# Fetched features and own parts copied to fixed places, and transfers moved, in a graph network on one Trainium2 core

## The reference

```python
def _agg(entity_emb, relation_emb, W, head, tail, edge_type):
    a_input = jnp.concatenate([entity_emb[head], entity_emb[tail]], axis=-1)
    e = jnp.sum(a_input @ W * relation_emb[edge_type], axis=-1)
    e = jax.nn.leaky_relu(e, LEAKY_SLOPE)
    m = jax.ops.segment_max(e, head, num_segments=n)
    ex = jnp.exp(e - m[head])
    alpha = ex / segment_sum(ex, head)[head]
    return segment_sum(entity_emb[tail] * alpha[:, None], head) + entity_emb
# twice: ent = l2_normalize(_agg(ent, ...)); res = 0.5 * res + ent
```

## Time and profile before

| | |
|---|---|
| median of 3 runs | 5385.7 us (5385.49 to 5385.82) |
| the profiled execution | 5347.59 us, span 5346.3 us |
| mean granted TensorE clock | 0.635 |
| busy: PE, DVE, ACT, POOL | 3116.6, 3511.7, 2114.8, 1815.5 us |
| stages (us of the span) | before the hops 0 to 1349, hop 0 to about 2710, hop 1 2763 to 4112, normalisation to 4142, GAT scores to 4203, GAT's loop 4245 to 4608, the rest to 5346 |

### The profile page before, as it was taken

The page is one execution under the profiler, slowest core; times in us unless marked ns, Lnnn a source line. Parts: engine busy times, 40 slices in busy tenths (PEclk is TensorE's granted clock), DMA queues, the critical chain, the costliest instruction groups (busy, mean ns, idle before and its releaser), DMA issues. The chain is left out here.

```text
span 5346.3 us, 64952 instructions
## 1 busy us (share of the span) xinstructions
PE 3116.6 (58%) x16252; PEld 2276.0 (43%) x16253; DVE 3511.7 (66%) x8740; ACT 2114.8 (40%) x5595; POOL 1815.5 (34%) x1836
## 2 busy tenths in 40 slices
PE   3288888867144444444533444444454388878877
PEld 0144444456143434343533343433343388734443
DVE  8888888823466666666845666666677498553444
ACT  0255555532344444444522222222232488522331
POOL 5000000070666666666026766666630000011210
PEclk6699999977555555555555555555555555588997
DMA  0000000030222222222011222222210300000000
GB/s 10 6 0 0 0 0 0 0 138 3 64 54 57 53 57 54 56 54 56 21 37 50 58 55 55 56 54 56 54 40 11 133 1 1 2 10 4 4 2 13
DMA packets 136619, 183.67 MB, mean 34 GB/s; under 512 B 48690, under 2 KB 110043, under 8 KB 135323
## 3 DMA queue, kind: packets, MB, share of 16 engines
q1 hardware_dynamic: 85404, 84.66, 5.8%
q0 software_dynamic: 50048, 77.77, 5.8%
q10 hardware_dynamic: 896, 18.10, 0.8%
HBM read 158.07 MB, written 22.34 MB: 34 GB/s over the span
## 5 line engine op out<-in xcount | busy, mean ns | idle before, releaser
L992 POOL DMA_INDIRECT adjacency<-dram_table,sorted_dst x1564 | 1565.6, 1001 | 1192.1 <-issue 484.9
L1016 PE MATMUL bank<-adjacency 128*128 x3520 | 779.3, 419 | 561.1 <-DMA adjacency<-dram_table,sorted_dst 298.4
L1016 PEld LDWEIGHTS bank<-adjacency 128*128 128x128 f32 x3520 | 759.1, 332 | 607.4 <-issue 607.4
L1061 ACT ACTIVATE adjacency<-adjacency 128x128 f32<-128x128 bf16 x1760 | 537.1, 394 | 56.7 <-issue 56.7
L1728 PE MATMUL bank<-adjacency,cheb_parts 128*128 128x512 f16 (+1 forms) x2100 | 437.5, 367 | 52.2 <-ACTq L95 31.4
L1088 DVE TENSOR_TENSOR adjacency<-adjacency,bank 128x2048 f32<-128x2048 f32 x110 | 251.6, 2287 | 306.5 <-remote 219.9
L1034 PE MATMUL bank<-ident,adjacency 128*128 128x128 f32 x440 | 149.5, 395 | 519.4 <-issue 519.3
L1048 ACT ACTIVATE adjacency<-adjacency 128x2048 f32<-128x2048 f32 x110 | 210.2, 1911 | 604.6 <-DVE adjacency L1088 603.0
L553 ACT ACTIVATE adjacency<-bank 128x400 f32 x590 | 296.9, 503 | 317.1 <-PE bank L525 312.0
L1997 POOL TENSOR_TENSOR cheb_y<-cheb_y,cheb_gain 128x512 f32<-128x512 f32 (+1 forms) x21 | 24.2, 1150 | 1154.7 <-DVE cheb_y L1913 1154.7
L522 PE MATMUL bank<-cell_hot,src_hot 128*128 128x400 f16 x1180 | 319.3, 353 | 74.2 <-DVE cell_hot L460 73.2
(11 more groups left out here) (448 smaller groups left out, 6754.2 us busy)
## 6 DMA issues: line engine op xcount, KB each, us to landing
adjacency<-dram_src_rows SPq DMA_DIRECT2D x440, 128.0 KB
adjacency<-dram_table,sorted_dst POOLq DMA_INDIRECT x1564
dram_adjacency<-adjacency ACTq DMA_DIRECT2D x1, 17600.0 KB, 44.4
adjacency<-dram_adjacency SPq DMA_DIRECT2D x1, 17600.0 KB, 46.1
dram_table<-adjacency SPq DMA_DIRECT2D x2, 1212.5 KB, 10.3
dram_nodes<-x_nodes SPq DMA_DIRECT2D x1, 800.0 KB, 4.5
x_nodes<-dram_nodes SPq DMA_DIRECT2D x1, 800.0 KB, 4.3
x_nodes<-in_x SPq DMA_DIRECT2D x1, 768.0 KB
```

Source lines behind the costliest of these rows:

```text
L992: pool.indirect_dma_start(ring[:, j % (RG * TG), :], None, dram["table"], bass.IndirectOffsetOnAxis(ap=S.dst_i[:, j:j + 1], axis=0)).then_ ...
L1016: ins = pe.matmul(sums[b % 2][:, s * W1:(s + 1) * W1], reach[:, b % 3, s, t, :], ring[:, bass.ds(at_r[s], TG), :][:, t, 0:W1], start=(t == ...
L1061: ins = act.activation(reach[:, b % 3, s, t, :], hot[:, b % 2, s, :, t], ACT.Identity, scale=-FAR, bias=score[:, b % 2, s * TG + t:s * TG ...
```

## The change

In a hop, ScalarE gets two stages more. One copies a batch's fetched features from the ring (65 of 97 columns, four tiles at once, 260 elements) into `carry`, two batches deep; the other copies the own parts' rows (96 elements) into `own_row`. The register reads go with them, and PE's matmuls read `carry` and `own_row` at fixed addresses. POOL's gate on the ring becomes `carried` instead of `summed`, and the ring shrinks from 44 to 42 groups. GAT's three weight loads are issued before hop 0 into places that last until GAT. The restore becomes two transfers: columns 18,450 to 80,000 of the arena before the normalisation behind hop 1, columns 9,600 to 18,450 behind the meeting; `squares` moves to the ring's start. In GAT's loop DVE forms the smaller of the two distances, ScalarE a Relu of it and, one step later, one Exp; DVE then multiplies by the counts.

```diff
-RG = 44
+RG = 42
@@ on_pool
-                pool.wait_ge(summed.sem, summed.at((g - RG + NB - 1) // SB))
+                pool.wait_ge(carried.sem, carried.at((g - RG + NB - 1) // SB))
@@ on_pe, sums
-                at_r = steps(pe, S.slots, (slice(0, 1),), b, RG * TG - TG)
-                for s in range(SB):
-                    g = min(b * SB + s, NG - 1)
-                    pe.wait_ge(tails[g % 8].sem, landed(g))
+                pe.wait_ge(carried.sem, carried.at(b))
...
-                                        ring[:, bass.ds(at_r[s], TG), :][:, t, 0:W1], start=(t == 0), stop=(t == TG - 1))
+                                        carry[:, b % 2, s, t, :], start=(t == 0), stop=(t == TG - 1))
@@ on_pe, lookups
-                at_j = blocks(pe, b)
                 pe.wait_ge(own_made.sem, own_made.at(b))
+                pe.wait_ge(own_rows.sem, own_rows.at(b))
...
-                                        row(own_parts[:, :, :], at_j[s]), start=True, stop=True)
+                                        own_row[:, b % 2, s, :], start=True, stop=True)
@@ on_act
-        for stage, b in lagged(batches, (5, 4, 3, 0, 2)):
+        for stage, b in lagged(batches, (5, 4, 3, 4, 1, 0, 2)):
...
+            elif stage == 3:
+                at_r = steps(act, S.slots, (slice(0, 1),), b, RG * TG - TG)
+                for s in range(SB):
+                    g = min(b * SB + s, NG - 1)
+                    act.wait_ge(tails[g % 8].sem, landed(g))
+                if b >= 2:
+                    act.wait_ge(summed.sem, summed.at(b - 2))
+                for s in range(SB):
+                    ins = act.activation(carry[:, b % 2, s], ring[:, bass.ds(at_r[s], TG), 0:W1], ACT.Copy)
+                ins.then_inc(carried.sem, 1)
+            elif stage == 4:
+                at_j = blocks(act, b)
+                if b >= 2:
+                    act.wait_ge(looked.sem, looked.at(b - 2))
+                for s in range(SB):
+                    ins = act.activation(own_row[:, b % 2, s, :], row(own_parts[:, :, :], at_j[s]), ACT.Copy)
+                ins.then_inc(own_rows.sem, 1)
@@ attention_hop
+    square_at = carver(arena, at)
+    part, square = acc[:, :, 0:D], square_at("squares", [P, NB, D], F32)
+    if hop == 1:
+        restore_rows(k, arena, dram, square_at.at(), NB * NPAD)
...
     k.meet("pe dve act pool sp")
+    if hop == 1:
+        restore_rows(k, arena, dram, start, square_at.at())
+def restore_rows(k, arena, dram, least, end):
+    kept = HELD * NPAD
+    k.sp.dma_start(arena[:, least:end], dram["adjacency"][:, least - kept:end - kept]).then_inc(k.sig("adjacency_restored", 16).sem, 16)
@@ layer_attention
+    load_gat_weights(k, dram, S)
     for hop in range(2):
         attention_hop(k, arena, region, cst, psum, dram, S, scores_w[:, :], x, ent, x if hop == 0 else ent, hop)
-    sp.dma_start(arena[:, region:], dram["adjacency"]).then_inc(restored.sem, 16)
@@ gat_act, "sum"
-                act.activation(near[:, i % 2, 0:w], rows[:, c % 2, 0, 0:w], ACT.Exp, scale=-1.0, bias=score[:, 0, a:a + 1])
-                act.activation(z[:, r, 0:w], rows[:, c % 2, 1, 0:w], ACT.Exp, scale=-1.0, bias=shallow[:, a:a + 1]).then_inc(exps.sem, 1)
+                if behind:
+                    exponent(*behind.popleft())
...
+                act.wait_ge(nearer.sem, nearer.at(i))
+                act.activation(z[:, i % R, 0:w], near[:, i % 2, 0:w], ACT.Relu, bias=scaled[:, 0, a:a + 1]).then_inc(gaps.sem, 1)
@@ gat_dve
+            dve.scalar_tensor_tensor(near[:, i % 2, 0:w], rows[:, c % 2, 0, 0:w], scaled[:, 1, a:a + 1], rows[:, c % 2, 1, 0:w],
+                                     ALU.subtract, ALU.min).then_inc(nearer.sem, 1)
...
-            dve.tensor_tensor(z[:, r, 0:w], z[:, r, 0:w], near[:, i % 2, 0:w], ALU.max).then_inc(larger.sem, 1)
-            dve.wait_ge(larger.sem, larger.at(i))
-            dve.scalar_tensor_tensor(z[:, r, 0:w], z[:, r, 0:w], 1.0, A[:, a, c * CW * P:c * CW * P + w], ALU.min, ALU.mult).then_inc(weighed.sem, 1)
+            dve.tensor_tensor(z[:, i % R, 0:w], z[:, i % R, 0:w], A[:, a, c * CW * P:c * CW * P + w], ALU.mult).then_inc(weighed.sem, 1)
```

More of the change, by code:

```diff
@@ L956, in hop_edges @@
     lane = carve("lane", [P, 2, SB, P], F32)
+    carry, own_row = S.carry, carve("own_row", [P, 2, SB, 3 * NREL], BF16)
     most, now, fade = carve("step_most", [P, SB], F32), carve("largest_now", [P, 2, SB], F32), carve("fade", [P, 3, SB], F32)
@@ L965, in hop_edges @@
     gaps, weighed, summed, added = k.sig("sum_gap"), k.sig("sum_weights"), k.sig("block_summed"), k.sig("block_added")
-    own_counted, counts = k.sig("own_counted"), k.sig("degree_added")
+    own_counted, counts, carried, own_rows = k.sig("own_counted"), k.sig("degree_added"), k.sig("rows_carried"), k.sig("own_rows")
     landed = lambda g: tails[g % 8].at(sum(tiles[g % 8:g + 1:8]) - 1)
@@ L1063, in on_act @@
                 ins.then_inc(reached.sem, 1)
-            elif hop == 0 and stage == 3:
+            elif stage == 3:
[15 more added lines that the diff above has]
+                ins.then_inc(own_rows.sem, 1)
+            elif hop == 0 and stage == 5:
                 at_g, at_j = steps(act, S.walk, (slice(0, 1), 0), b, TP - TG), blocks(act, b)
@@ L1254, in layer_attention @@
     S.step_count = keep("step_count", [P, BSTEPS], F32)
+    S.carry = keep("carry", [P, 2, SB, TG, D + 1], F32)
     scores_w = keep("scores_w", [D, 2 * NREL], F32)
@@ L1398, in gat_attention @@
         score_dve(k.dve)
-        weights.close(3)
+        for e in (k.act, k.pool, k.sp):
+            e.wait_ge(weights.sem, weights.at(2))
         for s in (turned, copied, made):
@@ L1410, in gat_attention @@
     near, z = sb("gat_near", [P, 2, CW * P], F32), sb("gat_z", [P, R, CW * P], F32)
[L1411 to L1414, removed]
+    scaled = sb("gat_scaled", [P, 2, NB], F32)
+    penalty, lowest, turned = k.sig("gat_penalty_made"), k.sig("gat_lowest"), k.sig("gat_low_turned")
+    scaled_made, diags, spread, rows_copied = k.sig("gat_scaled_made"), k.sig("gat_diags"), k.sig("gat_spread"), k.sig("gat_rows_copied")
+    nearer, gaps, exps, weighed, summed, evac = k.sig("gat_nearer"), k.sig("gat_gaps"), k.sig("gat_exps"), k.sig("gat_weighed"), k.sig("gat_summed"), k.sig("gat_evac")
     bank = lambda c, m: psum[(c % 2) * CW + m]
@@ L1437, in gat_act, with exponent @@
     def gat_act(act):
-        act.wait_ge(shallow_made.sem, shallow_made.at())
+        act.wait_ge(scaled_made.sem, scaled_made.at())
+        behind = collections.deque()
+        def exponent(i, w):
+            act.wait_ge(gaps.sem, gaps.at(i))
+            act.activation(z[:, i % R, 0:w], z[:, i % R, 0:w], ACT.Exp, scale=-1.0).then_inc(exps.sem, 1)
         for what, c, a in order():
@@ L1508, in gat_dve @@
             elif what == "sum":
+                nearest(c, a)
                 behind.append((c, a))
@@ L2225, in build @@
                 layer_gin(k, room(st), cst, psum, dram, A, x)
-        with ExitStack() as st:
-            layer_attention(k, cst, psum, dram, arena, x, S, room(st))
-        k.meet("pe dve act pool sp")
-        with ExitStack() as st:
-            layer_gat(k, room(st), cst, psum, dram, A, x)
+        with ExitStack() as later:
+            S.gat_w, S.gat_att = room(later)("gat_w", [D, D], F32), room(later)("gat_att", [P, 2, D], F32)
+            with ExitStack() as st:
+                layer_attention(k, cst, psum, dram, arena, x, S, room(st))
+            k.meet("pe dve act pool sp")
+            with ExitStack() as st:
+                layer_gat(k, room(st), cst, psum, dram, A, x, S)
         with ExitStack() as st:
```

45 lines of the change are left out of this document (25 added, 20 removed).

## The result

The changed kernel takes 5406.9 us (median of 6, 5405.4 to 5411.1); before, on the same chip, 5385.6 (6 runs): ratio 1.0042, 95% interval 1.0029 to 1.0055. It is slower by 21 us where 23 us faster was predicted. The wide range, 5322 to 5412, takes 5407 in, but it was stretched that far for rival R2, which didn't come about; that the time lies in it is luck. The profiled execution took 5408.8 us, span 5407.5, which is near its median; the one of before had been 38 us under the median of before. So the two traces stand 61 us apart and the medians 21, and no stage's difference between the two traces is to be taken for the change's without a second look.

A forecast was written before the change was run, and what follows sets the result against it. DVE's passes set the pace without gathers; during gathers a stretch delaying several engines made batches late. -35.8 + 2.2 + 13 - 2 = -22.6 from 5385.7 gave 5363 us, range 5322 to 5412 for 8 in 10.

The forecast's parts named there:

- R2: Hop 0: ScalarE's exp becomes late behind the counts; +97 us, about 5447, or +57, 5407; chance 0.17.
- The attention loop: GAT's loop: a step goes from 1.99 to 1.98 us, -2 us over 150 steps; bounds -16 and +15.
- R4: Attention loop: slower by the handing over between DVE and ScalarE, +15 us, 5380; chance 0.14.
- a step over 2.05 us: Attention loop: the sign that would show the loop slower by handing over between engines.
- Weights and restore: Behind hop 1: PE's wait for weights shrinks, -35.8 us; issue ahead of hop 0 costs +2.2; split restore stays hidden.
- Weights alone: Expectation for loads moved with the restore whole at its old place: -36 + 13, 2.2 for issue, about -20 us.
- the split's 13 us: Restore before the attention loop: issued whole at 4142, it would land at 4188 and take 13 us back.
- The hops: Hop 0: ScalarE's copies make batches 0.3 us later, x 44 = +13 us; bounds 0 and +97; hop 1 covered.
- the cover: Hop 0: ScalarE's 0.55 us idle before exp, against 2.7 us of new copies, leaving exp up to 2.2 late.
- theories P, C and D: Hop copies' gain: PE's table read and waits (-20 to -28); PE instructions removed (about -14); no ring reads or fewer instructions.
- R1: Hops: the gather stretch is relieved and PE's transposes close up; -82 us more, 5281; chance 0.13.
- The carried difference: Whole kernel: the profiled execution's 38.1 us below the median was carried over, 5325 profiled against 5363.

The follow-up runs named there:

- a1: The changed kernel with the attention loop of before, hop copies and moved transfers kept: 4974.4 us against 5007.1 for before, ratio 0.9933.
- a2: The changed kernel with the hops of before and RG 44, moved transfers and new loop kept: 5061.7 us, ratio 1.0111 to before.
- a3: The kernel before with the new attention loop alone: 5095.3 us, ratio 1.0177 to before.
- b3: The kernel before with the three weight loads ahead of hop 0, restore whole at its old place: 5351.6 us, ratio 0.9961 to before.
- b4: The kernel before with moved transfers and the new loop, nearest made one step ahead, hops of before: 5321.5 us, ratio 0.9906 to before.

## Why the prediction was wrong

**The attention loop: the step that failed.** It was forecast at -2 with a bound of +15 and measured +88. The working added nearest, relu, penalty, exp, multiply and low to 3.95 us and spread them over two steps. It took a cycle through the exponent and the multiplication, in which the delayed exp gives a step of slack, and overlooked the shorter one that has none: low waits for the penalty of the same step, nearest stands behind low, Relu waits for nearest, and the next penalty stands behind Relu. Those four edges are all within one step, at 0.74 + 0.67 + 0.84 + 0.62 = 2.87 us. Counting passes per engine (three and three, before and after) was right and told nothing. R4 had named the handing over, at 0.1 us a step and 15 in all, with the chance 0.14; its sign, a step over 2.05 us, came true. The size was nearly 0.9 in steps of one penalty, less over the loop, 90/175 = 0.5 on average, since the steps without a penalty lose next to nothing. The step of 1.99 us from which the prediction started holds for two steps of four; the other two take 2.14 and 2.85.

**Weights and restore: the size was right, one reason given for it wasn't.** -33.6 was forecast for both with their issue; -33 was measured with the hops' copies in (a1) and -34 without (a2 against a3), on a chip where the copies are neutral. Weights alone: -20 forecast, -21 measured; the split's 13 us as computed. The wait for the weights went whole, wherever they were moved. But the prediction took its 36 us to mean that the loads had not taken turns with the restore, and put the wait that turns would cost at about 2 us. The DMA queues of before decide this, q1 with the restore and q10 with the loads, from 4147 to 4178 and then from 4180 to 4188:

```profile
q1 hardware_dynamic: 363, 12.78, 97.6%
q10 hardware_dynamic: 360, 0.08, 1.2%
...
q1 hardware_dynamic: 96, 2.82, 81.5%
```

In the same 31 us 360 small packets and 363 large ones passed, one for one; the loads were in by 4179, 9 us before the restore (4142.1 + 46.1 = 4188.2). So they did take turns, and were late by it. By these figures a packet of the restore held one of the 16 DMA engines for some 1.3 us (31 x 16 x 0.976 / 363), and 368 small packets make 23 turns on each: an estimate of 30 us, and none passed in the first 5. (The Trainium skill, "DMA: Bandwidth & Descriptors", section "Issuing engines are not separate DMA queues", says that DMAs interleave whatever engine started them; this trace agrees, with 360 packets against 363. The prediction set the page aside for a price that it had put too low.) Either way the loads had to be moved ahead, and the number came out. Piece two took 14.4 us instead of the 5.8 given to it, as it was issued at 4148.14 behind piece one's last part, and still landed in time.

**The hops: +13 was forecast, -28 measured where the stretch is and nothing where it is not; R2's lateness didn't bind anywhere.** ScalarE's added work is smaller than forecast; its timeline in hop 0, to set beside the earlier trace rows, with DVE's L1104, for which exp (L1047) waits:

```profile
1931.08 2.29 DVE L1104 TENSOR_TENSOR adjacency<-adjacency,bank 128x2048 f32<-128x2048 f32 x1 [3.01 <-remote]
...
1933.86 0.19 ACT L1093 ACTIVATION_READ_ACCUMULATOR adjacency<-adjacency 128x1 f32 x1
1933.95 1.90 ACT L1047 ACTIVATE adjacency<-adjacency 128x2048 f32<-128x2048 f32 x1
...
1946.83 1.34 ACT L1071 ACTIVATE carry<-adjacency 128x260 f32 x4
1948.08 0.44 ACT L1078 ACTIVATE adjacency<-adjacency 128x96 bf16 x2
...
1950.45 0.28 ACT L1078 ACTIVATE adjacency<-adjacency 128x96 bf16 x1 [1.11 <-issue]
1951.89 0.30 ACT L1084 ACTIVATE step_src<-sorted_src,minus_block 128x4 bf16 x1 [1.16 <-issue]
1953.33 0.21 ACT L1085 ACTIVATE step_typ<-sorted_type 128x4 bf16 x1 [1.15 <-issue]
```

Four feature copies take 1.34 us, not 1.6, and two row copies 0.44, not 0.54. One copy lasts 0.41 and 0.27 as taken; in a row they overlap, which the sum left out. ScalarE is busy 221 us more in all (2336.0 against 2114.8), not 300. The last row copy stands in the stretch (1.11 us idle before it), and so do the step columns behind it (1.16 and 1.15). Exp starts at 1933.95, right behind the last count, 0.58 us after L1104 has ended. Over batches 5 to 44 of hop 0 this lateness is 0.60 us on average, where before had 0.03: the cover is used up, as forecast, but 0.6 us is late and not 2.2. Where the stretch is absent it is 0.03 with the copies too (a1). Nor is it seen in the batch's length. That the end of the stretch releases the batch, as the prediction held, fits this but is not shown by itself. POOL's burst begins 0.74 us behind the last turning transpose (L1040), as it did behind L1041, though the profile names "issue" there. The 0.3 us per batch taken for the copies is not there, and instead 0.29 are gained. PE's timeline in that same profile, to set beside the earlier trace rows:

```profile
1911.51 7.06 PE L1015 MATMUL bank<-carry,adjacency 128*128 128x65 f32 x32 [4.63 <-issue]
...
1919.65 0.44 PE L1033 MATMUL bank<-ident,adjacency 128*128 128x128 f32 x1
1920.48 0.37 PE L1033 MATMUL bank<-ident,adjacency 128*128 128x128 f32 x1 [0.39 <-issue]
1922.62 0.37 PE L1033 MATMUL bank<-ident,adjacency 128*128 128x128 f32 x1 [1.77 <-issue]
1924.80 0.37 PE L1033 MATMUL bank<-ident,adjacency 128*128 128x128 f32 x1 [1.81 <-issue]
1928.38 0.48 PE L1040 MATMUL bank<-ident,adjacency 128*128 128x128 f32 x1 [3.20 <-DVE adjacency L1191]
```

The sums take 7.06 us instead of 7.1, L1033's first two start 0.8 us apart, and the next 2.1 to 2.2, where 2.8 stood in the earlier trace rows. In this batch the turnings are less far apart; the stretch is there all the same. That PE has fewer instructions or waits to get through inside it is what theories P, C and D of the expectations share; it is argued, not shown, and none was told from the others. The Trainium skill, "SBUF — State Buffer", section "SBUF: two separate sides", holds that engine and DMA ports can't contend; the sums agree, with 7.06 us under gathers and the same 7.06 at 2602.75, behind the last gather, which speaks against seeking the 0.29 us in the operands' ports. R1, the relief of the stretch, had the chance 0.13 and a larger size (0.95 us a batch, not 0.29); its transposes didn't close up, and the gain came on one kind of chip alone.

Sum by the runs, on a chip with the stretch: -33 + 88 - 28 = +27; measured +21 and +26 (-33 and 88 are from a chip without it; the first two traces, with it, show the loop's loss at 90). On one without: -33 + 88 + 0 = +55; the change itself was not run there. R2 had named 5407 for exp 1.3 us late; that this is the time measured is a coincidence.

**The carried difference.** The prediction moved the 38 us between the profiled execution and the median along unexamined. By b3's trace some 20 of them may lie in the batches, the place where the change acts; the rest is open. The forecast of the median didn't rest on them, the reading of the two traces did.

## What to carry to other kernels

When a pass is moved from one engine to another, write out every cycle of waits and of instruction order within one step, and take the longest; busy time per engine is the floor, and one handing over placed behind a wait of the same step cost 0.9 us in each step that made a penalty here. The remedy was to make the handed-over value one step ahead, which turned +55 into -51. A small transfer of many packets beside a large one on another queue got one packet through for each of the large one's, and its 0.08 MB took 36 us; count packets, not bytes, move it ahead, and split the large one around its readiness.

## What the runs showed of the hardware

The same program differs by 7 to 8% between chips (or occasions, as each round had a chip of its own): before takes 5386 and 5372 us on one or two and 4999 to 5007 on four. Nearly the whole difference lies in the hops. b4 and a2 have the same hops and transfers; PE's first weighted matmul behind the hops comes 363 us later in b4, and the medians of before on these two chips differ by 365:

```profile
4165.75 0.66 PE L1396 MATMUL bank<-gat_w,gat_xt 64*128 64x64 f32 x2 [0.32 <-ACT gat_xt L1383]
```

```profile
3803.10 0.66 PE L1396 MATMUL bank<-gat_w,gat_xt 64*128 64x64 f32 x2 [0.32 <-ACT gat_xt L1383]
```

308 of the 363 us lie between the first and the last batch of each hop, the other 55 ahead of the first ones. Where before is slow PE's and ScalarE's single instructions stand 1.4 to 2.8 us apart while a burst of indirect DMAs is under way, and a batch takes 24.4 us where it takes 21.1 on the other. The granted clock of the hops is 0.50 to 0.52 on both. The 0.29 us a batch that the copies gain were seen only there. What makes the stretch was not found.

Two transfers on different queues shared the DMA engines packet by packet, 360 of one against 363 of the other in 31 us, though the first had 0.08 MB in them and the second 12.78.
